# A conditioned recurrence on one core: b2 turned early, W2 loaded in 1024-column pieces two at a time, whole products for its last piece, layer shares 8 5 5 7 7

## The reference, cut to what matters

```python
# x: (2, 1024, 256), cond: (2, 256), W1: (256, 256), W2: (256, 4096), b2: (4096,), rank 8
ae    = layernorm(cond) * g + b
h     = gelu(ae @ w1 + b1)
xw    = h @ w2 + b2                              # (2, 4096)
x_a, x_b = split(xw, 2); reshape to (2, 256, 8)
layer = base + einsum('bdr,bkr->bdk', x_a, x_b)  # a 256x256 matrix for each of 2 batch rows
y     = x + (x + x @ layer)
xW    = y @ Wx + b
h_t   = tanh(h_{t-1} @ Wh + xW_t)                # t = 0..1023, h_{-1} = cond
out   = y + h_t
```

## Time and profile before

| | us |
|---|---|
| median of 3 runs | 763.08 (762.8 to 763.83) |
| the profiled execution | 763.37 |
| its span in the profile | 761.5 |

### The profile page before, as it was taken

The page is one execution under the profiler, slowest core; times in us unless marked ns, Lnnn a source line. Parts: engine busy times, 40 slices in busy tenths (PEclk is TensorE's granted clock), DMA queues, the critical chain, the costliest instruction groups (busy, mean ns, idle before and its releaser), DMA issues.

```text
span 761.5 us, 46019 instructions
## 1 busy us (share of the span) xinstructions
PE 694.1 (91%) x18824; PEld 627.9 (82%) x18824; DVE 281.7 (37%) x1546; ACT 500.6 (66%) x5151; POOL 6.2 (1%) x18
## 2 busy tenths in 40 slices
PE   6999999999999999999999999999999999999997
PEld 5888888888888888888888888888888888888886
DVE  6533333333333333333333333333333333333332
ACT  6666666666666666666666666666666666666665
POOL 3000000000000000000000000000000000000000
DMA  8000000000000000000000000000000000000000
GB/s 284 7 8 8 11 11 9 11 7 9 11 11 9 11 8 8 11 11 9 11 9 7 11 11 9 11 9 7 11 11 9 11 10 7 10 11 9 7 8 6
DMA packets 12118, 12.38 MB, mean 16 GB/s; under 512 B 1785, under 2 KB 11012, under 8 KB 11656
## 3 DMA queue, kind: packets, MB, share of 16 engines
q1 hardware_dynamic: 11840, 9.46, 4.1%
q0 software_dynamic: 64, 0.00, 0.0%
q10 hardware_dynamic: 8, 0.00, 0.0%
HBM read 7.36 MB, written 2.10 MB: 12 GB/s over the span
## 4 chain that ended last, share of the span: by engine, by line
PE 76%; ACT 19%; issue 2%; DMA 1%; DVE 1%; SPq 0%
PE acc L350 49%; ACT h_pre L544 19%; PE pre L350 15%; PE pre L323 4%; PE p_w L307 4%; PE p_w L302 2%; DMA w_f<-w_dram 1%; PE p_w L295 1%; PE pre L320 1%; PE acc L455 1%; DVE w_s L812 0%; SPq L229 0%; ACT w_s L603 0%; PE p_w L475 0%; ACT lay_s L558 0%
## 5 line engine op out<-in xcount | busy, mean ns | idle before, releaser
L350 PE MATMUL acc<-h_pre,wh_s 128*128 128x2 f16 x8184 | 379.5, 167 | 57.1 <-ACT h_pre L544 0.2
L544 ACT ACTIVATE h_pre<-pre 128x2 f16<-128x2 f32 x2046 | 240.6, 169 | 247.3 <-PE pre L350 245.1
L350 PEld LDWEIGHTS acc<-h_pre,wh_s 128*128 128x128 f16 x8184 | 296.2, 105 | 120.7 <-ACT h_pre L544 104.5
L713 DVE TENSOR_TENSOR h_lo<-p_f,h_pre 128x4 f16<-128x4 f32 x1024 | 166.1, 162 | 458.5 <-ACT p_f L550 453.6
L350 PE MATMUL pre<-h_rnd,wh_s 128*128 128x2 f16 x4088 | 273.9, 171 | 0.0
L350 PE MATMUL acc<-h_lo,wh_s 128*128 128x2 f16 x4092 | 257.3, 167 | 0.0
L350 PEld LDWEIGHTS pre<-h_rnd,wh_s 128*128 128x128 f16 x4088 | 191.5, 109 | 0.0
L350 PEld LDWEIGHTS acc<-h_lo,wh_s 128*128 128x128 f16 x4092 | 189.0, 106 | 0.1
L554 ACT ACTIVATE h_f<-acc 128x4 f32<-128x4 f32 x1023 | 185.4, 181 | 0.5 <-PE acc L350 0.5
L552 ACT ACTIVATE h_rnd<-acc 128x4 f16<-128x4 f32 x1021 | 172.5, 169 | 0.0
L550 ACT ACTIVATE p_f<-acc 128x4 f32<-128x4 f32 x1022 | 161.5, 158 | 0.0
(11 more groups left out here) (109 smaller groups left out, 156.8 us busy)
## 6 DMA issues: line engine op xcount, KB each, us to landing
w_f<-w_dram SPq DMA_DIRECT2D x2, 1024.0 KB, 9.1
x_in<-x_dram SPq DMA_DIRECT2D x32, 64.0 KB, 2.3
out_dram<-o_row SPq DMA_DIRECT2D x64, 32.0 KB, 1.9
w_f<-w_dram SPq DMA_DIRECT2D x3, 512.0 KB, 6.1
w_f<-w_dram SPq DMA_DIRECT2D x3, 256.0 KB, 10.0
base_f<-base_dram SPq DMA_DIRECT2D x1, 256.0 KB, 10.0
wh_f<-wh_dram SPq DMA_DIRECT2D x1, 256.0 KB, 10.1
wx_f<-wx_dram SPq DMA_DIRECT2D x1, 256.0 KB, 10.2
```

Of the source, the lines that this page charges most:

```text
L350: return nc.tensor.matmul(dst, wh_s[:, pw, ki, mo * P:(mo + 1) * P], h[:, par, ki, :], start=False, stop=True, skip_group_check=True)
L544: nc.scalar.activation(h_pre[:, n % 2, m, :], src, func, scale=scale).then_inc(s_hpre[(n // HALF) % 2], 1)
L713: nc.vector.tensor_sub(h_lo[:, par].rearrange("p m b -> p (m b)"), p_f[:, 0:COLS], h_pre[:, par].rearrange("p m b -> p (m b)")).then_inc(s ...
```

## The change

Five edits, in the opening and in the shares of the steps:

1. SP issues b2 ahead of the first W2 load.
2. W2 is loaded in eight pieces of 1024 columns (512 KB) instead of seven loads of three sizes, each with its own semaphore. From the third piece on SP waits, before it issues piece n, until piece n-2 has landed. x's first block is issued behind the fourth piece, and base, Wh and Wx behind the last.
3. PE turns b2 right behind the condition and does two of the four zero products there. The other two, and the zero product into `acc[0]`, stand ahead of the W1 products. DVE seeds `acc[0]` ahead of its first `w2_low`.
4. ACT and DVE still split the last piece in two halves of 512 columns (`W2_PARTS`), but PE multiplies it whole, once both halves are there: 8 + 8 products of 128 weight columns instead of 32 of 64.
5. The shares of layer products at u = 9 to 13 are 8, 5, 5, 7, 7 instead of 7, 7, 7, 7, 4.

```diff
-        W2_LOADS = [(0, 0, P), (1, 0, P), (0, P, 3 * P), (1, P, 3 * P), (0, 3 * P, 4 * P),
-                    (1, 3 * P, 3 * P + P // 2), (1, 3 * P + P // 2, 4 * P)]
-
-        W2_PIECES = [(0, 0, 0, P), (1, 0, 1, P), (2, 1, 0, P), (2, 2, 0, P), (3, 1, 1, P), (3, 2, 1, P), (4, 3, 0, P),
-                     (5, 3, 1, P // 2), (6, 3, 1, P)]
+        W2_PIECES = [(q, k) for q in range(4) for k in range(NM)]
+
+        W2_PARTS = [(q, k, 0, P) for q, k in W2_PIECES[:-1]] + [(3, 1, 0, P // 2), (3, 1, P // 2, P)]
...
+        LAYER_SHARE = (0, 8, 13, 18, 25, 32)
...
+            sync.dma_start(b2_q[:, :], b2.rearrange("(q n) -> q n", q=4)).then_inc(s_b2, 16)
             load_w2(0)
             sync.dma_start(w1_f[:, :, :], w1.rearrange("(k p) n -> p k n", p=P)).then_inc(s_w1, 16)
-            sync.dma_start(b2_q[:, :], b2.rearrange("(q n) -> q n", q=4)).then_inc(s_b2, 16)
-            for n in range(1, len(W2_LOADS)):
+            for n in range(1, len(W2_PIECES)):
+                if n >= 2:
+                    sync.wait_ge(s_w2[n - 2], 16)
                 load_w2(n)
-                if n == 2:
+                if n == 3:
                     sync.dma_start(x_in[:, :], x_rows[0:BLOCK]).then_inc(s_xload, 16)
...
-                            product = layer_products(share(LAYER, 7, u - LAYERS - 1))
+                            begin, end = LAYER_SHARE[u - LAYERS - 1:u - LAYERS + 1]
+                            product = layer_products(LAYER[begin:end])
...
+            pe.wait_ge(s_zero, 1)
+            pe.wait_ge(s_b2, 16)
+            for r in range(RANK):
+                nc.tensor.transpose(acc[1][:, 64 + 4 * r:64 + 4 * (r + 1)],
+                                    b2_q[:, :].rearrange("q (p r) -> q r p", r=RANK)[:, r, :], ident[0:4, 0:4])
+            pe.wait_ge(s_ones, 3)
+            zeros = ab_st[:, :].rearrange("p q b s r -> p (q b s r)")
+            for k in range(NM):
+                nc.tensor.matmul(pre[B][:, 0, k * D:(k + 1) * D], ident16[:, :], zeros, start=k == 0,
+                                 stop=True, skip_group_check=True)
             pe.wait_ge(s_vec, 48)
             nc.tensor.transpose(p_w[:, 64:64 + 3 * NM], vec_r[:, :], ident[0:3 * NM, 0:3 * NM]).then_inc(s_turn0, 1)
...
             pe.wait_ge(s_ae, 1)
+            nc.tensor.matmul(acc[0][:, 64:64 + P], ident16[:, :], zeros[:, 0:P],
+                             start=True, stop=True, skip_group_check=True).then_inc(s_b2turn, 1)
+            for k in range(NM):
+                marked = nc.tensor.matmul(pre[B][:, 1, k * D:(k + 1) * D], ident16[:, :], zeros, start=k == 0,
+                                          stop=True, skip_group_check=True)
+            marked.then_inc(s_mark, 1)
             pe.wait_ge(s_w1, 16)
...
-            for n in range(len(W2_PIECES)):
-                _, q, k, d, part = piece(n)
+            for n, (q, k) in enumerate(W2_PIECES):
                 if n == 2:
                     turn_x()
                 for pw, ready in ((0, s_w2hi), (1, s_w2lo)):
-                    pe.wait_ge(ready, n + 1)
+                    pe.wait_ge(ready, n + 1 if n < len(W2_PIECES) - 1 else len(W2_PARTS))
```

More of the change, by code:

```diff
@@ L120, in cond_recurrence @@
         s_cond, s_vec, s_w1, s_b2, s_base = sem("s_cond"), sem("s_vec"), sem("s_w1"), sem("s_b2"), sem("s_base")
-        s_w2 = [sem(f"s_w2_{n}") for n in range(7)]
+        s_w2 = [sem(f"s_w2_{n}") for n in range(4 * NM)]
         s_wh, s_wx, s_b, s_bw = sem("s_wh"), sem("s_wx"), sem("s_b"), sem("s_bw")
@@ L163, in cond_recurrence @@
         s_xhi0, s_yhi0, s_ylo0, s_yrest = sem("s_xhi0"), sem("s_yhi0"), sem("s_ylo0"), sem("s_yrest")
+        s_zero = sem("s_zero")
         s_laysum, s_mark, s_basein = sem("s_laysum"), sem("s_mark"), sem("s_basein")
@@ L178, in cond_recurrence, with columns @@
         s_own = sem("s_own")
-        W2_LOADS = [(0, 0, P), (1, 0, P), (0, P, 3 * P), (1, P, 3 * P), (0, 3 * P, 4 * P),
-                    (1, 3 * P, 3 * P + P // 2), (1, 3 * P + P // 2, 4 * P)]
-        W2_PIECES = [(0, 0, 0, P), (1, 0, 1, P), (2, 1, 0, P), (2, 2, 0, P), (3, 1, 1, P), (3, 2, 1, P), (4, 3, 0, P),
-                     (5, 3, 1, P // 2), (6, 3, 1, P)]
[L188 to L192, removed]
+        W2_PIECES = [(q, k) for q in range(4) for k in range(NM)]
+        W2_PARTS = [(q, k, 0, P) for q, k in W2_PIECES[:-1]] + [(3, 1, 0, P // 2), (3, 1, P // 2, P)]
+        def columns(q, d0=0, d1=P):
+            return slice((q * P + d0) * RANK, (q * P + d1) * RANK)
         x_rows = x.rearrange("b t (m p) -> t m b p", p=P)
@@ L226, in load_w2 @@
             def load_w2(n):
-                k, d0, d1 = W2_LOADS[n]
-                part = slice(d0 * RANK, d1 * RANK)
-                sync.dma_start(w2_f[:, k, part], w2[k * P:(k + 1) * P, part]).then_inc(s_w2[n], 16)
+                q, k = W2_PIECES[n]
+                sync.dma_start(w2_f[:, k, columns(q)], w2[k * P:(k + 1) * P, columns(q)]).then_inc(s_w2[n], 16)
             sync.dma_start(cond_r[:, :], cond).then_inc(s_cond, 16)
             sync.dma_start(vec_r[2 * NM:3 * NM, :], b1.rearrange("(m p) -> m p", p=P)).then_inc(s_vec, 16)
+            sync.dma_start(b2_q[:, :], b2.rearrange("(q n) -> q n", q=4)).then_inc(s_b2, 16)
             load_w2(0)
             sync.dma_start(w1_f[:, :, :], w1.rearrange("(k p) n -> p k n", p=P)).then_inc(s_w1, 16)
-            sync.dma_start(b2_q[:, :], b2.rearrange("(q n) -> q n", q=4)).then_inc(s_b2, 16)
-            for n in range(1, len(W2_LOADS)):
+            for n in range(1, len(W2_PIECES)):
+                if n >= 2:
+                    sync.wait_ge(s_w2[n - 2], 16)
                 load_w2(n)
-                if n == 2:
+                if n == 3:
                     sync.dma_start(x_in[:, :], x_rows[0:BLOCK]).then_inc(s_xload, 16)
@@ L450, in _ @@
                 for pw, ready in ((0, s_w2hi), (1, s_w2lo)):
-                    pe.wait_ge(ready, n + 1)
+                    pe.wait_ge(ready, n + 1 if n < len(W2_PIECES) - 1 else len(W2_PARTS))
                     for r in range(RANK):
                         c = 64 + (q * RANK + r) * 2 * NB
-                        w = w2_s[:, pw, k, part].rearrange("p (d r) -> p r d", r=RANK)
-                        last = nc.tensor.matmul(acc[0][d, c:c + 2 * NB], w[:, r, :],
+                        w = w2_s[:, pw, k, columns(q)].rearrange("p (d r) -> p r d", r=RANK)
+                        last = nc.tensor.matmul(acc[0][:, c:c + 2 * NB], w[:, r, :],
                                                 hid_s[:, k].rearrange("p s b -> p (s b)"),
@@ L600, in w2_high @@
             def w2_high(n):
-                load, q, k, d, part = piece(n)
-                act.wait_ge(s_w2[load], 16)
+                q, k, d0, d1 = W2_PARTS[n]
+                part = columns(q, d0, d1)
+                act.wait_ge(s_w2[min(n, len(W2_PIECES) - 1)], 16)
                 nc.scalar.copy(w2_s[:, 0, k, part], w2_f[:, k, part]).then_inc(s_w2hi, 1)
@@ L617, in high @@
                                      scale=SCALE).then_inc(s_hi, 1)
-            for n in range(1, len(W2_PIECES)):
+            for n in range(1, len(W2_PARTS)):
                 w2_high(n)
@@ L781, in linked @@
                 dve.wait_ge(s_link, count[0])
-            nc.vector.memset(acc[1][0:NB * 4 * RANK, 0:NB * BLOCK], 0.0)
+            nc.vector.memset(acc[1][0:NB * 4 * RANK, 0:NB * BLOCK], 0.0).then_inc(s_zero, 1)
             dve.wait_ge(s_cond, 16)
@@ L809, in w2_low @@
             def w2_low(n):
-                load, q, k, d, part = piece(n)
+                q, k, d0, d1 = W2_PARTS[n]
+                part = columns(q, d0, d1)
                 dve.wait_ge(s_w2hi, n + 1)
                 nc.vector.tensor_sub(w2_s[:, 1, k, part], w2_f[:, k, part], w2_s[:, 0, k, part]).then_inc(s_w2lo, 1)
-            w2_low(0)
             dve.wait_ge(s_b2turn, 1)
@@ L820, in _ @@
             seeded.then_inc(s_b2seed, 1)
+            w2_low(0)
             dve.wait_ge(s_hidhi, 1)
```

## The result

| | before | after |
|---|---|---|
| median of 6 runs each, us | 763.51 (762.8 to 763.83) | 766.59 (765.95 to 767.59) |
| ratio after to before | | 1.0043, interval 1.0032 to 1.0053 |
| the profiled execution, us | 763.37 | 766.31 |
| its span, us | 761.5 | 764.5 |
| first tanh of the steps begins at, us | 27.57 | 30.55 |

Span less first tanh is 733.9 us in both: all of the loss lies in the opening, as far as the profile resolves.

A forecast was written before the change was run, and what follows sets the result against it. The PE/ACT recurrence bounds the kernel; in the opening, PE's backlog delays the reduce. W2's loading and whole products together gain 2.2 us, b2 and shares zero: 763.37 becomes 761.2 profiled, median 760.9, range 759.9 to 762.8.

The forecast's parts named there:

- I take 3.15: Opening, W2 loads: time of one 512 KB piece from issue to landing, taken between 2.8 and 3.4 us; 3.2 with SP's wake.
- L: Opening: landing time of W2's last piece, second piece's landing plus three trips; forecast 17.9 us, gain 20.1 - L.
- The lower end, 2.8: Shortest trip of a W2 piece: the condition's 1.47 us for 2 KB plus 512 KB at 402 GB/s, 1.3 us.
- The other end: Longest trip of a W2 piece: x's quiet load gave 3.8 us, its page median 2.3 gave 3.4, which was used.
- Slower by the same mechanism: Rival for W2's loads: SP's wait replaces PE's backlog; at 4.2 us a trip, 1.5 us lost, 764.6; chance 0.06.
- The path behind the landing: Opening, after W2's last piece: ACT's half casts, Wx's cast, then DVE's L826; the reduce starts 3.15 us after that landing.
- Whole products: Opening, PE on W2's last piece: 16 products replace 32, 3.5 us become 1.1; reduce at 21.2, 2.0 us earlier.
- b2 early: Opening: b2 turned early and zero products moved; zero effect, 0.5 us lost only if DVE is the bound.
- the shares: Steps u = 9 to 13, layer products 8 5 5 7 7: zero effect, the eighth product fitting at u = 9.
- The ceiling set by DVE's own work, 20.05: Opening: earliest start of the reduce that DVE's work from 10.73 on allows, 20.05, a gain of 3.2 us.
- x's block behind the waits: Opening: x's first block, issued behind SP's waits, is needed by PE only behind the second piece; nothing added.
- base, Wh, Wx behind the waits: Opening: three loads behind W2's last piece land 0.65 us apart, Wx 2.0 us after it, just in time; nothing added.

## Why the prediction was wrong

The sign was wrong, and one number of it made it so.

- *The step that failed* is the term "I take 3.15" for a trip. A trip was 3.8 us alone and 4.5 to 5.4, 5.0 on average, in the last three links of the changed kernel's chain. The second piece landed at 7.96, even a little before the 8.3 taken; the three trips behind it, with their wakes, took 23.16 - 7.96 = 15.2 us instead of 9.6. That is 5.6 us more; the second piece's early landing gives 0.3 of it back, which makes L 5.3 us late, and the path behind it another 0.1. The profiled execution came out at 766.31 instead of 761.2, 5.1 late: the one term is the whole miss.
- *Why the term was too small.* The lower end, 2.8, took the latency of a load of 2 KB and added the data at the full queue's rate. The lone trip shows what that leaves out: its data takes 2.4 us, not 1.3, with about 1.1 us of slow packets at its head. The other end was worked out as 3.8 from x's quiet trip, which is what a lone piece measures (by a sum that left the slow start out, so the match is in part luck), and then put back to 3.4 by the page's median of x. And neither end held anything for the other piece under way, though the sentence before had asked for just that. The nearest row was the first load of W2, 512 KB in 4.2 us, with W1 and the second piece issued right behind it; it was told as a rival and set aside as a thing of the start. It is the low end of what was found.
- *By the Trainium skill's* fit (DMA: Bandwidth & Descriptors, Anatomy of one DMA), 2.0 us and the bytes over 436 GB/s, a trip of 512 KB is 3.2; the runs measure 3.8 alone, and the measurement decides. The Trainium skill's rule (same page, Bandwidth) to batch to 1 MiB or more pointed the right way in so far as it puts more bytes under way: two loads of 1 MB lose nothing, while one of 1 MB is as slow as two of 512 KB.
- *The rivals.* "Slower by the same mechanism", with 0.06, is what happened. Its point of decision (a trip of 3.9, L = 20.1) was right; its price was too low, since it had taken 4.2 and not 4.5 to 5.4. Two of the signs of being wrong that the prediction named came: long trips, and ACT waiting for W2 at the end.
- *The path behind the landing* was right: L + 3.15 forecast, 26.22 - 23.16 = 3.06 measured. The 3.24 with one under way is Wx's landing.
- *Whole products*: 2.0 us by the rows, with the reduce at 21.2; alone they bring 2.4 (interval 1.5 to 3.1, from the ratio's), with the reduce at 21.33. Right.
- *b2 early* and *the shares*: zero forecast, nothing measured beyond the noise. The eighth product fits, right. For the case where DVE is the bound the prediction had 0.5 us lost by the early b2; the traces point the other way: DVE's second low part starts at 10.28 to 10.42 with it (alone, in the changed kernel, without waits and with four under way), at 10.73 before. The ceiling set by DVE's own work, 20.05, was reckoned from 10.73 and came out 0.3 too late: with four under way the reduce is at 19.79.
- *x's block behind the waits*: forecast as not waited for. PE did wait, 0.99 us, and turned x at 13.44; by 15.3 it had caught up and waited for DVE again, so it cost nothing. The forecast was wrong, the zero right.
- *base, Wh, Wx behind the waits*: forecast just in time, landing 0.65 us apart with Wx at L + 2.0. Wx landed at L + 2.0 (25.17) and its cast ended at 25.85, L + 2.7. Right here; with one and with three under way Wx is what ends last.

Four kernels split the sum in two ways, from the queued pieces with half products, 763.1, to the changed kernel, 766.6: the waits first, +4.7, and then the whole products, -1.2; or the whole products first, -2.6 to 760.6, and then the waits, +6.0 (b2 and the shares change with the products). Not all of the -2.6 is the products': alone they moved the reduce by 1.9, here it moves by 2.7, from 23.23 to 20.49, and DVE starts its second low part at 10.42 instead of 11.16, since that piece landed earlier and b2 was turned early. How much of the rest each of the two is worth is open. The whole products' gain is smaller behind the waits since the landing then hides PE's backlog.

A version that beats both is the changed kernel without its waits, 760.57 us, or with four pieces under way, 760.16, or with two of 1 MB, 760.72. The three can't be told apart by these runs.

## What to carry to other kernels

Before a wait is put between loads, work out the bytes under way: the stream goes at bytes under way over trip, and the trip has to be taken from a row with as many bytes under way as the new kernel will have. A trip built from a small transfer's latency and the full queue's rate comes out too short: here it gave 2.8 us, 1.0 less than a lone trip and 1.7 to 2.6 less than one with company. And sometimes a forecast's sign hangs on one duration that no row shows, here 3.15 against the 3.9 at which it turns. Then the range must reach to the nearest row of the same size (here 512 KB in 4.2 us), and that end must get more than a small chance.

## What the runs showed of the hardware that was not expected

- A load of 512 KB from SP is 3.7 to 3.9 us from issue to landing with no other piece beside it. In the trip shown 1.0 passes before its first packet and 0.4 after its last, and the first 1.1 us between them run at 137 GB/s on average, the rest at 290.
- Two loads under way hold each other up: 4.5 to 5.4 us each in the changed kernel's chain, where one alone has 3.8. Going from one to two raises the rate from 138 to 236 GB/s, three give 353, and it takes 2 MB under way to reach the 400 of a full queue.
- What makes the slow start, and what the loads share while they hold each other up, no run here tells apart; it stays open.
